# Softmax sums gathered by DMA to 128x64, inverted there and spread back to the denominators' rows, with a new order of the fill

## The chip, the core and the metric

The kernel is one program on one core of a Trainium2 chip. The metric is device time in microseconds, from launch to the end of the last store; less is better. The core has a matrix engine (TensorE, PE in the rows; PEld is its weight loading), three engines for elementwise work (VectorE is DVE, ScalarE is ACT, GpSimd is POOL), a queue engine that issues the transfers (SyncE, SP), and 16 DMA engines that carry them. All engines run at once and wait for each other by semaphores. Each engine takes its own instructions strictly in the order in which they are written.

## The reference, cut to what matters

One transformer block, post-norm, on x of 32 x 256 x 128 in float32: 16 heads of width 8, a causal mask with a linear decay, and a gated feed-forward part with three more layers of width 512.

```python
Q, K, V = (split_heads(x @ W.T + b) for W, b in ((Wq, bq), (Wk, bk), (Wv, bv)))
scores = einsum('bhid,bhjd->bhij', Q, K) / sqrt(8)
scores = where(causal_mask, -inf, scores) - delta      # delta = i - j
out = einsum('bhij,bhjd->bhid', softmax(scores, axis=-1), V)
x = layernorm(x + out @ Wo.T + bo)
h = silu(tlin(x, w1)) * tlin(x, w2)
h = gelu(tlin(gelu(tlin(h, h1)), h2))                  # exact gelu
x = layernorm(x + tlin(h, w3))
```

## The kernel before, in words

The 32 sequences are taken two at a time: 16 pairs, `q` = 0 to 15, of 512 tokens; `b` is the sequence within the pair. Work on one pair is a chain of steps, and the kernel runs three pairs staggered: in **slot** t (t = 2 to 15) the attention of pair t runs beside the projection and the gate layers of pair t-1 and the wide layers of pair t-2. Before the slots stands a **fill** (pairs 0 and 1 from nothing), after them a **drain**. For every engine there is a hand-written list of steps for the fill (`PE_FILL`, `ACT_FILL`, ...), for a slot (`PE_ORDER`, ...; the last number in an entry is the pair relative to t) and for the drain. The lists are unrolled in that order, so they alone decide what stands behind what on an engine.

The steps that matter here, by their names in the lists:

- `qq`, `qk`, `qv`: projections of x, all in one PSUM bank. `qhi`, `qlo` split q and k into a rounded part and a remainder; `qstack`, `kstack` are the seven transfers that lay these parts into the stacks `qs`, `ks`, 32 rows a head. For pair 0 they go half by half (seven transfers for b = 0, seven for b = 1).
- `s` (b, n), n = 0 to 7: scores of two heads (L622, L625) into two of four score banks. `smax` (L947) on VectorE takes the row maximum of each; that frees the banks. In the fill, b = 1 of pair 0 and all of pair 1 go one head at a time through two other banks: `s1` (L638, L640) and `smax1` (L959). I call these first-maxima.
- `mT`, `mTc`, `mTl`, `mTd`: the maxima are transposed, split into two parts and sent by DMA into rows of `qs`, so that the next product already has them subtracted.
- `st` (b, n): the scores again, transposed, minus the maximum (L663, L665), into the four banks; `exp` (L798) on ScalarE writes `pt` and frees them; `sel` (L1094) on GpSimd zeroes what the mask forbids.
- `pv` (b, u), u = 0 to 3: `pt` times V and a column of ones (L682), so that the bank holds numerators in its even rows and the row sums in its odd rows, eight copies of each sum. `araw` (L806 on ScalarE or L983 on VectorE) copies the bank to `raw`, 128 x 512.
- `repack` (L557): eight transfers for a pair and half a batch each: odd rows of `raw` to `den`, even rows to `num`, so that numerator and denominator of an element lie in one partition. `arec` (L987) inverts `den` for b on VectorE, 128 x 256; `amul` (L1120) on GpSimd multiplies to `attT`; `wo` (L691) on TensorE is the projection. It waits for both halves of `attT`.
- `res1`, `lnstat`, `rstd`, `lnnorm`, `x1t`, `x1hi`, `x1lo`, `x1c`: residual, layer norm, transpose and splitting.
- `g`, `u` (m = 0 to 3): the two gate layers (L577, L583; in the fill also L579 with the weights' remainder), `tanh`, `gate`, `gmul`, `ghi`, `glo` make the gated product's two parts. `h` (layer, m): the wide layers, four matmuls with the rounded part and four with the remainder; `gelu`, `hhi`, `hlo` (L1140) follow each. `w3h`, `w3l`, `zt`, `res2`, `lnstat 2`, `store` end a pair.

Between fill and slots TensorE reads a flag that says whether the weights have a remainder at all (L761, `lo_flag`); here they have none, and the slots run without these matmuls. The flag needs `w_hi`, `w_lo` and `w_mx`, which split the weights on ScalarE, split on GpSimd and take the largest remainder on VectorE.

`x_tok` and `xT` are the pair's input in its two layouts (`tload`, `xload`).

## Time and profile before

| what | us |
|---|---|
| median of 3 runs (lowest to highest) | 791.47 (790.95 to 791.99) |
| the profiled execution's own time | 791.65 |
| its span, first to last instruction | 789.8 |
| TensorE busy | 730.5 (92%) |
| VectorE busy | 632.0 (80%) |
| ScalarE busy | 553.2 (70%) |
| GpSimd busy | 510.6 (65%) |
| mean granted clock of TensorE | 0.95 of full |

The profiled execution lies within the runs. Busy times are sums over the whole span; they don't say which engine ends a stage. That is read from stretches of the trace and from what ended an engine's idle time. The end of a matmul is modelled: a gap of a few tenths of a microsecond behind one can be covered by it, and then shows only as a late start of the next.

### The profile page before, as it was taken

How to read it: one execution, taken by the hardware profiler on the slowest of the kernel's cores; microseconds unless marked ns; L12 is line 12 of the kernel's file. 1: busy time of each engine (PE TensorE's matmuls, PEld its weight loads, DVE VectorE, ACT ScalarE, POOL GpSimd, SP SyncE). 2: the span in 40 equal slices, each digit the busy share in tenths (PEclk: the TensorE clock that was granted, in tenths of full speed). 3: DMA queues.
4: the chain of work that ended last, by engine and by line, in shares of the span. 5: the costliest groups of instructions: out<-in, count | busy, mean ns of one | idle time of the engine just before them, and what ended most of it. 6: DMA issues, size and time to landing. Idle time of an engine off the chain costs nothing. (4 is left out here: it accounts for less than half of the span.)

```text
span 789.8 us, 18746 instructions
## 1 busy us (share of the span) xinstructions
PE 730.5 (92%) x6026; PEld 500.7 (63%) x6026; DVE 632.0 (80%) x2759; ACT 553.2 (70%) x874; POOL 510.6 (65%) x616
## 2 busy tenths in 40 slices
PE   3587789999999999999999999999999999999995
PEld 1365457676766667676766667676766667676663
DVE  3796679798988979798988979798988979798232
ACT  3154456959687685959687685959687785959684
POOL 2084356766758586766758586766758586767864
PEclk8557699999999999999999999999999999999998
DMA  7311030402112030302112130402112130300100
GB/s 208 138 58 44 0 133 10 140 15 101 55 57 99 34 116 10 139 16 100 55 62 94 39 112 8 139 16 100 55 61 94 41 112 7 127 15 18 40 1 28
DMA packets 36778, 53.28 MB, mean 67 GB/s; under 512 B 5288, under 2 KB 16872, under 8 KB 36680
## 3 DMA queue, kind: packets, MB, share of 16 engines
q1 hardware_dynamic: 36680, 52.07, 19.3%
q8 instruction: 50, 0.82, 0.4%
q14 instruction: 48, 0.39, 0.2%
HBM read 12.20 MB, written 4.19 MB: 21 GB/s over the span
## 5 line engine op out<-in xcount | busy, mean ns | idle before, releaser
L947 DVE CUSTOM_DVE_ANT_0 ps<-ps,causal 128x256 f32<-128x256 f32 (+1 forms) x928 | 297.3, 389 | 22.2 <-PE ps L625 20.4
L798 ACT ACTIVATE pt<-ps 128x768 f32<-128x768 f32 x256 | 195.7, 812 | 37.2 <-PE ps L665 33.6
L1094 POOL TENSOR_SCALAR_AFFINE_SELECT pt<-pt 128x512 f32<-128x512 f32 x256 | 160.3, 637 | 93.5 <-ACT pt L798 89.5
L1140 POOL TENSOR_TENSOR hlo<-hf,hhi 128x512 fp32r<-128x512 f32 x128 | 164.7, 1288 | 85.7 <-ACT hhi L881 85.7
L871 ACT ACTIVATE hf<-ps,vec_sb 128x512 f32<-128x512 f32 x128 | 86.2, 684 | 101.5 <-PE ps L583 100.9
L577 PE MATMUL ps<-hhi,h_hi 128*128 128x512 f32 x496 | 145.8, 415 | 0.3 <-ACT hhi L881 0.3
L583 PE MATMUL ps<-hlo,h_hi 128*128 128x512 f32 x496 | 136.4, 396 | 0.2 <-POOL hlo L1140 0.2
L947 DVE DVE_READ_ACCUMULATOR2_ANT m<- 128x1 f32 x928 | 127.6, 138 | 0.0
L583 PEld LDWEIGHTS ps<-hlo,h_hi 128*128 128x128 f32 x496 | 93.4, 188 | 22.9 <-POOL hlo L1140 0.6
L682 PE MATMUL ps<-pt,vst 128*32 128x256 f32 (+1 forms) x2048 | 106.2, 337 | 1.1 <-POOL pt L1094 1.1
L577 PEld LDWEIGHTS ps<-hhi,h_hi 128*128 128x128 f32 x496 | 85.3, 188 | 22.1 <-issue 3.0
L881 ACT CAST hhi<-hf 128x512 fp32r<-128x512 f32 x128 | 79.3, 620 | 3.9
L622 PE MATMUL ps<-ks,qs 32*128 32x256 f32 x464 | 72.4, 386 | 9.7 <-DVE m L947 8.4
L682 PEld LDWEIGHTS ps<-pt,vst 128*32 128x32 f32 x2048 | 56.1, 111 | 37.7 <-issue 5.3
L1146 POOL TENSOR_TENSOR hlo<-hf,hhi 128x512 fp32r<-128x512 f32 x60 | 76.9, 1282 | 3.3 <-ACT hhi L820 2.5
L622 PEld LDWEIGHTS ps<-ks,qs 32*128 32x128 f32 x464 | 37.9, 185 | 50.6 <-issue 24.5
L663 PE MATMUL ps<-qs,ks 32*128 32x128 f32 x512 | 65.1, 331 | 2.7 <-DMA qs<-mT_lo 1.6
L665 PE MATMUL ps<-qs,ks 32*128 32x256 f32 x512 | 66.5, 340 | 0.0
L663 PEld LDWEIGHTS ps<-qs,ks 32*128 32x128 f32 x512 | 39.7, 189 | 42.2 <-ACT pt L798 22.8
L577 PE MATMUL ps<-x1hi,w_hi 128*128 128x512 f32 x128 | 63.7, 497 | 1.3 <-DVE sg L1024 1.1
L1037 DVE SCALAR_TENSOR_TENSOR hf<-ps,half_s,sg 128x512 f32<-128x512 f32 x60 | 44.9, 748 | 23.4 <-PE ps L583 21.8
L987 DVE RECIPROCAL den<-den 128x256 f32<-128x256 f32 x32 | 55.8, 1745 | 8.2 <-DMA num<-raw 8.2
(116 smaller groups left out, 1154.4 us busy)
## 6 DMA issues: line engine op xcount, KB each, us to landing
qs<-q_hi SPq DMA_DIRECT2D x30, 256.0 KB
ks<-k_hi SPq DMA_DIRECT2D x30, 256.0 KB
xT<-in_x SPq DMA_DIRECT2D x16, 256.0 KB, 2.8
x_tok<-in_xtok SPq DMA_DIRECT2D x16, 256.0 KB, 3.2
den<-raw SPq DMA_DIRECT2D x64, 64.0 KB, 2.0
num<-raw SPq DMA_DIRECT2D x64, 64.0 KB, 2.0
out<-o_tok SPq DMA_DIRECT2D x16, 256.0 KB, 2.0
qs<-q_lo SPq DMA_DIRECT2D x15, 256.0 KB
```

The costliest lines, as they stand in the source:

```text
L577: pe.matmul(acc, w_hi[name][:, col[k]:col[k] + P], hi(k), start=(k == 0), stop=False)
L583: last = pe.matmul(acc, w_hi[name][:, col[k]:col[k] + P], lo(k), start=False, stop=(k == n - 1))
L622: pe.matmul(ps[:, bank, 0:T], qr[:, P:T], kr, start=True, stop=False, skip_group_check=True)
L663: pe.matmul(ps[:, bank, 0:P], kr[:, P:T], qr[:, P:T], start=True, stop=False, skip_group_check=True)
L682: last = pe.matmul(acc, vst[p][:, 2 * b + kb, u, c, :], pr, start=(kb == 0 and not odd), stop=(kb == 1 and odd == 1), skip_group_check=True)
L798: nc.scalar.activation(pt[u][:, c:c + 2, :], ps[:, first:last + 1, 0:3 * P], ACT.Exp).then_inc(t_free.sem, 1)
L871: nc.scalar.activation(hf[:, n % 4, :], ps[:, FB[m % 2], :], ACT.Gelu, scale=vec_sb[:, col:col + 1]).then_inc(f_gelu.sem, 1)
L881: nc.scalar.copy(h_hi[layer % 2][:, m, :], hf[:, n % 4, :]).then_inc(hhi_ready.sem, 1)
L947: part = nc.vector.tensor_tensor_reduce(ps[:, bank, cols], ps[:, bank, cols], mask, 1.0, LOWEST, ALU.add, ALU.max, m32[b][:, it, c + e, u: ...
L1094: nc.gpsimd.affine_select(out=diag, in_=diag, compare_op=ALU.is_ge, fill=0.0, base=0, pattern=[[0, 2], [0, 2], [1, P]], channel_multiplier ...
L1140: nc.gpsimd.tensor_tensor(h_lo[layer % 2][:, m, :], hf[:, n % 4, :], h_hi[layer % 2][:, m, :].bitcast(F32), ALU.subtract).then_inc(hlo_rea ...
L1146: nc.gpsimd.tensor_tensor(lo[:, m, :], gated(q, m), hi[:, m, :].bitcast(F32), ALU.subtract).then_inc(h0lo_ready.sem, 1)
```

## The change

`raw` holds eight copies of each row sum. Before, all eight are moved and all are inverted: a reciprocal over 128 x 256 for each b. Now a `gather` takes every eighth row from row 1 of `raw` for each half, 16 rows of 256 elements, and lays them as 64 x 64 into a new tile `sums` (one for each b, 128 x 64 with two copies of each sum). `arec` inverts `sums`. Four `spread` transfers copy all of `sums` into every fourth row of `den`, once for each residue of the row number. `repack` moves the numerators alone. `araw` waits for repack and gather of the half before it, `arec` for the gather, `spread` for the reciprocal, and `amul` for repack and spread.

The core of the diff (an order table's line or two stand for the tables):

```diff
 SP_ORDER = [
-    ("repack", 0, 1, 0, -1), ("tload", -1), ("repack", 0, 1, 1, -1), ("repack", 0, 0, 0, -1),
+    ("gather", 0, 0, -1), ("gather", 0, 1, -1), ("repack", 0, 0, -1), ("repack", 0, 1, -1),
+    ("spread", 0, 0, -1), ("spread", 0, 1, -1), ("spread", 0, 2, -1), ("spread", 0, 3, -1),
...
+        sums = [sb(f"sums{b}", [P, T // 4]) for b in range(2)]
...
-        repacked = Signal("repacked", 8, 16)
+        gathered = [Signal(f"gathered{b}", 2, 16) for b in range(2)]
+        repacked = [Signal(f"repacked{b}", 2, 16) for b in range(2)]
+        spread = [Signal(f"spread{b}", 4, 16) for b in range(2)]
...
+                    elif kind == "gather":
+                        _, b, half = s
+                        raw_ready.wait(sp, q, b + 1)
+                        spread[b].wait(sp, q - 1)
+                        carry(sp, "sp")
+                        sp.dma_start(sums[b][64 * half:64 * half + 64, :],
+                                     raw[1::8, half * T:(half + 1) * T]).then_inc(gathered[b].sem, 16)
                     elif kind == "repack":
-                        _, b, odd, half = s
+                        _, b, half = s
                         raw_ready.wait(sp, q, b + 1)
                         attT_ready.wait(sp, q - 1, b + 1)
                         carry(sp, "sp")
-                        sp.dma_start((num, den)[odd][64 * half:64 * half + 64, b * T:(b + 1) * T],
-                                     raw[odd::2, half * T:(half + 1) * T]).then_inc(repacked.sem, 16)
+                        sp.dma_start(num[64 * half:64 * half + 64, b * T:(b + 1) * T],
+                                     raw[0::2, half * T:(half + 1) * T]).then_inc(repacked[b].sem, 16)
+                    elif kind == "spread":
+                        _, b, row = s
+                        rec_ready.wait(sp, q, b + 1)
+                        attT_ready.wait(sp, q - 1, b + 1)
+                        carry(sp, "sp")
+                        sp.dma_start(den[row::4, b * T:(b + 1) * T], sums[b][:]).then_inc(spread[b].sem, 16)
...
-                        repacked.wait(dve, q - 1 + b, 8 - 4 * b)
+                        repacked[1 - b].wait(dve, q - 1 + b)
+                        gathered[1 - b].wait(dve, q - 1 + b)
...
-                        repacked.wait(dve, q, 4 * b + 4)
-                        nc.vector.reciprocal(den[:, b * T:(b + 1) * T], den[:, b * T:(b + 1) * T]
-                                             ).then_inc(rec_ready.sem, 1)
+                        gathered[b].wait(dve, q)
+                        nc.vector.reciprocal(sums[b][:], sums[b][:]).then_inc(rec_ready.sem, 1)
...
-                        rec_ready.wait(pool, q, b + 1)
+                        repacked[b].wait(pool, q)
+                        spread[b].wait(pool, q)
```

All order tables are new. The slot's boundary is turned by about one gate block: `u 3`, `gate 3` and `gmul 3` of pair t-1 now stand at the start of slot t+1, while `ghi 1` to `ghi 3`, `araw 1` and the first three `gelu`/`hhi` on ScalarE stand at the end of slot t. On ScalarE, `("table", "exp")` now stands ahead of the first k copy of the fill, and `w_hi 1` behind `qhi 1, 1`; on GpSimd, `w_lo 1` stands behind `sel 0, 4` of pair 1.

TensorE at the start of the fill. L638 and L640 are first-maxima of b = 1, L622 and L625 two-head steps of b = 0 (L643, L646 in the changed file, whose lines lie about 21 further down). Before:

```order
L596 MATMUL ps<-xT,wq_sb 128x512
L638 MATMUL ps<-ks,qs 128x256
L640 MATMUL ps<-ks,qs 128x128
L638 MATMUL ps<-ks,qs 128x256
L640 MATMUL ps<-ks,qs 128x128
L622 MATMUL ps<-ks,qs 128x256 x2
```

After:

```order
L617 MATMUL ps<-xT,wq_sb 128x512
L643 MATMUL ps<-ks,qs 128x256 x2
L646 MATMUL ps<-ks,qs 128x128 x2
L643 MATMUL ps<-ks,qs 128x256 x2
L646 MATMUL ps<-ks,qs 128x128 x2
L643 MATMUL ps<-ks,qs 128x256 x2
```

Three two-head steps of the first half now stand ahead of the first step of the second half.

TensorE at the start of the first slot (every later slot is alike). L577 and L583 with `hhi` and `hlo` are `h 1, 0`; L682 is `pv`. Before, behind the flag:

```order
L622 MATMUL ps<-ks,qs 128x256 x2
L625 MATMUL ps<-ks,qs 128x128 x2
L682 MATMUL ps<-pt,vst 32x256 x4
L682 MATMUL ps<-pt,vst 32x128 x4
L622 MATMUL ps<-ks,qs 128x256 x2
L625 MATMUL ps<-ks,qs 128x128 x2
L622 MATMUL ps<-ks,qs 128x256 x2
L625 MATMUL ps<-ks,qs 128x128 x2
L682 MATMUL ps<-pt,vst 32x256 x4
L682 MATMUL ps<-pt,vst 32x128 x4
L577 MATMUL ps<-hhi,h_hi 128x512 x4
```

After:

```order
L598 MATMUL ps<-x1hi,w_hi 128x512
L604 MATMUL ps<-x1lo,w_hi 128x512
L643 MATMUL ps<-ks,qs 128x256 x2
L646 MATMUL ps<-ks,qs 128x128 x2
L643 MATMUL ps<-ks,qs 128x256 x2
L646 MATMUL ps<-ks,qs 128x128 x2
L703 MATMUL ps<-pt,vst 32x256 x4
L703 MATMUL ps<-pt,vst 32x128 x4
L703 MATMUL ps<-pt,vst 32x256 x4
L703 MATMUL ps<-pt,vst 32x128 x4
L643 MATMUL ps<-ks,qs 128x256 x2
L646 MATMUL ps<-ks,qs 128x128 x2
```

`u 3` has come in front, the first two score steps stand together, and so do the two `pv` steps.

SyncE in a slot, from the first transfer out of `raw`. Before:

```order
L557 DMA den<-raw 64x256
L519 DMA x_tok<-in_xtok 128x512
L557 DMA den<-raw 64x256
L557 DMA num<-raw 64x256 x2
L557 DMA den<-raw 64x256 x2
L557 DMA num<-raw 64x256 x2
L550 DMA qs<-mT_hi 4x4x256
```

After:

```order
L565 DMA sums<-raw 64x1x64 x2
L572 DMA num<-raw 64x256 x2
L579 DMA den<-sums 32x4x64 x4
L565 DMA sums<-raw 64x1x64 x2
L572 DMA num<-raw 64x256 x2
L579 DMA den<-sums 32x4x64 x4
L500 DMA xT<-in_x 128x512
L527 DMA x_tok<-in_xtok 128x512
L558 DMA qs<-mT_hi 4x4x256
```

The four spreads of b = 0 stand ahead of the gathers of b = 1, and the loads of x behind all of them.

## Rows read from the trace of the kernel before

**Rows 1.** The page: TensorE and exp; 40 equal slices, busy and granted clock in tenths.

```profile
PE 730.5 (92%) x6026; PEld 500.7 (63%) x6026; DVE 632.0 (80%) x2759; ACT 553.2 (70%) x874; POOL 510.6 (65%) x616
...
PE   3587789999999999999999999999999999999995
...
PEclk8557699999999999999999999999999999999998
...
L798 ACT ACTIVATE pt<-ps 128x768 f32<-128x768 f32 x256 | 195.7, 812 | 37.2 <-PE ps L665 33.6
```

**Rows 2.** Busy time by stage: stretch, length, engines (instructions), granted clock, DMA share, GB/s.

```profile
0.00:22.80 22.80, 7.71 (x21) 4.09 (x22) 6.47 (x30) 7.99 (x15) 4.90 (x13) 0.83 0.69 206
22.80:80.50 57.70, 42.71 (x345) 30.17 (x344) 47.92 (x253) 23.25 (x35) 27.31 (x32) 0.59 0.21 72
80.50:112.30 31.80, 25.95 (x201) 15.93 (x200) 20.73 (x54) 16.27 (x26) 12.47 (x21) 0.74 0.22 78
112.30:733.90 621.60, 610.51 (x5268) 418.87 (x5268) 538.54 (x2376) 470.48 (x742) 430.94 (x519) 1.00 0.19 66
733.90:789.80 55.90, 43.66 (x196) 31.66 (x196) 18.29 (x46) 35.23 (x58) 34.99 (x34) 0.94 0.04 15
```

**Rows 3.** Timeline of the fifth slot's start: start, length, engine, line, operation [idle before].

```profile
289.82 0.38 PE L622 MATMUL ps<-ks,qs 32*128 32x256 f32 x2
...
291.62 2.62 POOL L1146 TENSOR_TENSOR hlo<-hf,hhi 128x512 fp32r<-128x512 f32 x2
...
291.90 0.38 PE L622 MATMUL ps<-ks,qs 32*128 32x256 f32 x2 [0.48 <-DVE m L947]
...
293.88 1.10 SPq L557 DMA_DIRECT2D den<-raw  x2
294.09 1.10 PE L583 MATMUL ps<-hlo,h_hi 128*128 128x512 f32 x4
...
295.12 0.39 PE L622 MATMUL ps<-ks,qs 32*128 32x256 f32 x4
...
298.36 1.75 DVE L987 RECIPROCAL den<-den 128x256 f32<-128x256 f32 x1
...
300.32 0.75 POOL L1120 TENSOR_TENSOR attT<-num,den 128x256 f32<-128x256 f32 x1
...
302.23 1.16 PE L691 MATMUL ps<-wo_sb,attT 128*128 128x128 f32 x8
```

**Rows 4.** Timeline of the same slot's middle: gate block, transpose, two transposed score steps.

```profile
320.49 0.50 PE L577 MATMUL ps<-x1hi,w_hi 128*128 128x512 f32 x1
...
320.83 0.39 PE L583 MATMUL ps<-x1lo,w_hi 128*128 128x512 f32 x1
...
321.37 0.39 PE L649 MATMUL ps<-ident,m 128*16 128x128 f32 x2 [0.16 <-DVE k_lo L919]
...
321.69 0.33 PE L663 MATMUL ps<-qs,ks 32*128 32x128 f32 x2
...
322.16 0.33 PE L663 MATMUL ps<-qs,ks 32*128 32x128 f32 x2
```

**Rows 5.** The reciprocals' line, and the landing of the transfers of L557.

```profile
L987 DVE RECIPROCAL den<-den x32: 1740/1744/1755, 75.2 to 740.6; 128x256 f32<-128x256 f32 x32
...
DMA to landing us min/median/max: 1.9/2.0/4.2
```

**Rows 6.** Timeline of the fill: half 0's last stack transfer, first scores, last first-maximum, first slot.

```profile
15.17 0.61 SPq L540 DMA_DIRECT2D ks<-k_lo  x1
...
21.96 0.65 PE L638 MATMUL ps<-ks,qs 32*128 32x256 f32 x2 [8.24 <-DMA qs<-no_max]
...
85.68 0.58 PE L638 MATMUL ps<-ks,qs 32*128 32x256 f32 x1
...
112.30 0.38 PE L622 MATMUL ps<-ks,qs 32*128 32x256 f32 x2 [1.09 <-DVE lo_flag L1066]
```

**Rows 7.** The transfers' table: target, source, count, KB, issue to landing in us.

```profile
x<-in_h SPq DMA_DIRECT2D x1, 256.0 KB, 6.7
```

More of the change, by code:

```diff
@@ L91 @@
-    ("exp", 0, 5, 1), ("exp", 0, 6, 1), ("lnnorm", 1, 0), ("x1hi", 0), ("x1c", 0), ("tanh", 0, 0),
-    ("qhi", 0, 2), ("exp", 0, 7, 1), ("tanh", 1, 0), ("qhi", 1, 2), ("ghi", 0, 0), ("tanh", 2, 0),
-    ("ghi", 1, 0), ("exp", 1, 0, 1), ("exp", 1, 1, 1), ("exp", 1, 2, 1), ("tanh", 3, 0), ("exp", 1, 3, 1),
-    ("exp", 1, 4, 1), ("exp", 1, 5, 1), ("exp", 1, 6, 1), ("ghi", 2, 0), ("exp", 1, 7, 1), ("table", "gelu", 1),
+    ("qhi", 0, 0), ("table", "exp", -1), ("qhi", 1, 0), ("rows", 0), ("w_hi", 0), ("qhi", 0, 1), ("qhi", 1, 1),
@@ L95 @@
+    ("lnnorm", 1, 0), ("exp", 1, 0, 1), ("exp", 1, 1, 1), ("x1hi", 0), ("x1c", 0), ("exp", 1, 2, 1),
+    ("exp", 1, 3, 1), ("tanh", 0, 0), ("tanh", 1, 0), ("exp", 1, 4, 1), ("ghi", 0, 0), ("exp", 1, 5, 1),
+    ("tanh", 2, 0), ("exp", 1, 6, 1), ("exp", 1, 7, 1), ("ghi", 1, 0), ("tanh", 3, 0), ("ghi", 2, 0),
+    ("ghi", 3, 0), ("araw", 1, 1), ("gelu", 1, 0, 0), ("hhi", 1, 0, 0), ("gelu", 1, 1, 0), ("hhi", 1, 1, 0),
+    ("gelu", 1, 2, 0), ("hhi", 1, 2, 0),
 ]
 DVE_FILL = [
-    ("rows", 0), ("qlo", 0, 0), ("qlo", 1, 0), ("vadd", 0), ("smax1", 1, 0, 0, 0), ("smax", 0, 0, 0),
@@ L157 @@
+    ("ghi", 0, -1), ("exp", 0, 6, 0), ("exp", 0, 7, 0), ("tanh", 2, -1), ("exp", 1, 0, 0), ("table", "exp", 0),
+    ("exp", 1, 1, 0), ("exp", 1, 2, 0), ("tanh", 3, -1), ("exp", 1, 3, 0), ("exp", 1, 4, 0), ("exp", 1, 5, 0),
+    ("exp", 1, 6, 0), ("exp", 1, 7, 0), ("ghi", 1, -1), ("ghi", 2, -1), ("ghi", 3, -1), ("araw", 1, 0),
+    ("gelu", 1, 0, -1), ("hhi", 1, 0, -1), ("gelu", 1, 1, -1), ("hhi", 1, 1, -1), ("gelu", 1, 2, -1),
+    ("hhi", 1, 2, -1), ("table", "gelu", 0),
 ]
 DVE_ORDER = [
-    ("smax", 0, 0, 0), ("smax", 0, 1, 0), ("smax", 0, 2, 0), ("arec", 0, -1), ("smax", 0, 3, 0),
@@ L201 @@
+    ("ghi", 1, -1), ("tanh", 3, -1), ("ghi", 2, -1), ("ghi", 3, -1), ("table", "exp", 0), ("gelu", 1, 0, -1),
+    ("hhi", 1, 0, -1), ("gelu", 1, 1, -1), ("hhi", 1, 1, -1), ("gelu", 1, 2, -1), ("hhi", 1, 2, -1),
+    ("gelu", 1, 3, -1), ("hhi", 1, 3, -1), ("table", "gelu", 0), ("table", "exp", 1), ("gelu", 2, 0, -1),
+    ("hhi", 2, 0, -1), ("gelu", 2, 1, -1), ("hhi", 2, 1, -1), ("table", "gelu", 1), ("gelu", 2, 2, -1),
+    ("hhi", 2, 2, -1), ("gelu", 2, 3, -1), ("hhi", 2, 3, -1),
 ]
 DVE_DRAIN = [
-    ("arec", 0, -1), ("arec", 1, -1), ("res1", -1), ("lnstat", 1, -1), ("x1lo", -1), ("gate", 0, -1),
```

135 lines of the change are left out of this document (65 added, 70 removed), and 99 rows, old and new, of tables (DVE_FILL, PE_DRAIN, PE_FILL, PE_ORDER).

## The prediction

> **What bounds the kernel now.** I read the head of the page first. TensorE is busy 92% of the span, and the slices show where it is not: the first seven and the last one. The granted clock is at its lower level (1.2 GHz, half) through slices 2 to 4 and full (2.4 GHz) afterwards [rows 1]. The table by stages turns this into three parts [rows 2]: a fill of 112.3 us with 76.4 us of TensorE work, fourteen slots of 44.4 us (621.6 us, 11.1 us idle in all, 0.8 us a slot), and a drain of 55.9 us. VectorE is busy 538.5 of the 621.6 us of the slots, 87%. So the slots are TensorE's. A VectorE instruction that gets cheaper there pays only where TensorE waits for it. The fill is another matter: 36 of its 112 us are idle TensorE and much of the rest ran at half clock.
>
> Some waiting in the slots is hidden, because a matmul's modelled end covers the gap behind it. Two adjacent score steps run side by side in 0.4 us (the row at 295.12, four heads). At a slot's start the step at 291.90 waits 0.48 us for VectorE. In the middle, the step at 321.69 and its partner at 322.16 start 0.47 us apart instead of together, because ScalarE's exp holds the bank, and the transpose at 321.37 comes 0.3 us later than the pace of the two matmuls before it (320.49 and 320.83) allows [rows 3, 4]. I count about 2.5 us a slot of such gaps. That is the most that the slots can give: 35 us.
>
> **The change, part by part.**
>
> 1. *Reciprocals.* 32 at 1.744 us go [rows 5]. Their form after is 128x64. One of 128x4 elements on the same engine is not a reciprocal, so I bound the new one below by a quarter of the old, 0.44 us, and above by the old 1.74; I take 0.5, since the old one costs 6.8 ns an element in its row, far more than any start-up. VectorE sheds 32 x 1.25 = 40 us. In a slot both reciprocals stand behind a score step that VectorE finished and before one that TensorE has not yet delivered: the second ran 298.36 to 300.1, and the next scores came with the pair at 299.42. Nothing in the slots waited for it, so this alone is worth 0 to 0.5 us a slot.
>
> 2. *Eight transfers for b become four plus four, with a reciprocal between.* SyncE issues at 0.55 us each (293.88, two in 1.10) and a transfer lands 2.0 us after its issue, 1.9 at best and 4.2 at worst [rows 3, 5]. Before, raw to attention for the second half took: issue at 293.88, product at 300.32 to 301.1, projection at 302.23 [rows 3]. After, counted from the end of the last score-transposed step of the slot before (st, n=7; 289.82 in these rows): the four pv steps and the moved u(3) put raw at 3.6 to 4.2; the gathers are issued to 5.5 and land at 6.9; the reciprocal ends at 7.4; four spreads are issued by 9.9, the last lands at 11.3; the product follows on GpSimd behind hlo(1,1), 11.55 to 12.3. The projection is due on TensorE at 13.5. The relay is longer by about one landing and eight issues in all, and it is **hidden with 1.4 us to spare**. SyncE issues 30 transfers a slot instead of 22, 17 us of 44; the loads that now stand behind the spreads (x for the next pairs, the maxima, the stacks) are due 5 us or more later. The other half is gathered before the slot turns and its spread lands at 4.6; GpSimd takes it at 7.4. Cost: 0.
>
> 3. *The slot is turned.* u(3), gate, product and hi copy of the fourth gate block cross the slot's boundary. Start of the slot, time 0 as above: pv 0 to 0.79, u(3) to 1.36, s(0),s(1) to 2.0 (the exp of the last bank ends at 1.6), two pv to 3.5, s(2) at 3.65 when VectorE has done s(0) behind the moved product, h(1,0) from 4.0. GpSimd now has three lo parts behind its last masking instead of two: sel to 2.35, then three at 1.23 us to 6.06. In the trace the pair (291.62, 2.62 us) ended at 294.24, just after the matmuls that need it had begun at 294.09 [rows 3]. h(1,0) therefore waits 0.35 us for the third and ends at 6.4. Before, the same work took 5.30 (289.82 to 295.12) plus 1.22 for the pv and u that came ahead: 6.5. Gain 0.1 us. In the middle u(1) moves ahead of g(1), so a block of two matmuls, 0.34 us from 320.49 to 320.83 and some 0.23 for the second, fills the gap before the transpose and the exp wait between 320.83 and 322.16; later two steps wait 0.06 and 0.2 us for exp that did not. Gain 0.3 us. **Slots: 0.4 us x 14 = 5.6 us.** The bounds are -0.8 us a slot (both new waits of 0.35 us, plus one like that at 291.90) and +1.2 (0.1 and 0.3, and the 0.8 us idle of today gone).
>
> 4. *The fill, start.* TensorE's first score step now belongs to half 0, not half 1. Today it waits 8.24 us, to 21.96, for the last of fourteen stack transfers. The seventh, the last of half 0, is issued at 15.17 and finished at 15.78 [rows 6], so it lands at about 17.5. The load of xT for pair 1 is now issued after the five weight loads; the last weight load took 6.7 us to land after an issue at 9.19 (its row gives 6.7) [rows 7], so xT comes near 16.5 and its projection ends at 17.6 to 18.7. I take 18.0 for the first scores: 4.0 us early.
>
> 5. *The fill, until the last first-maximum.* VectorE has 47.9 us of work in the 57.7 us behind 22.8 [rows 2] and is the pacemaker. Doing pair 0's eight two-head steps first, TensorE keeps it fed; of its 9.8 idle us there I give back a quarter, 2.5. The exps of pair 0 begin 6.6 us earlier, the last one 7.5 us earlier. Then some is given back: the second reciprocal waits for pv, raw, the gathers (2.6 us), and its four spreads and product take 4.9 us more before the projection of pair 0. The last first-maximum, at 85.68 today [rows 6], comes at about 81.5: **4.2 us early**.
>
> 6. *The fill, tail.* From that step to the first score step of the slots at 112.30 it takes 26.6 us today [rows 6]. After, VectorE does LN statistics, q_lo, and the maxima's two copies, the transfer lands, and the exps of pair 1's second half start at +7. ScalarE then holds eight exps (0.81 in their row, 0.75 back to back) [rows 1], two copies (1.1), three tanh and a hi copy (2.5), with one 2 us wait for the second gate block, to +19.7; the last g ends at +19.6, the weight flag costs 1.4 (1.09 of it is the wait in the row at 112.30), and u(3) is already in: the slot's s(0) is at +22. Gain 4.6 us. **Fill: 4.2 + 4.6 = about 9 us.** Bounds 3 (the tail gains nothing and one us is lost in 5) and 14 (the 7.5 us are kept). Two extra table loads, 1.28 us each, stand behind raw in the fill and before an exp that is due 2.8 us later: nothing.
>
> 7. *The drain.* Of its 55.9 us TensorE works 43.7 [rows 2]. The third lo part costs h(1,0) 1.2 us where no scores hide it; the projection, which waited 0.44 us for attention, then does not. Together 0 to +1; I take 0.
>
> **Sum** on the profiled execution: 791.65 (span 789.8 and 1.85 around it) - 9 - 5.6 = **777.0 us**. The median of the runs, 791.47, is 0.2 lower, which changes nothing.
>
> **A rule and a row.** The rows have only transfers of 1 KB pieces between on-chip tiles, landing at 2.0 us [rows 5]; gather and spread move pieces of 256 bytes. The Trainium skill, "DMA: Bandwidth & Descriptors", Specifications, says that below 512 B a DMA engine does read-modify-write. The same page, "Why small descriptors are slow (HBM only)", says that copies inside SBUF don't suffer from small descriptors. By the second the sum stands as it is; by the first it is rival B. No row of before tells them apart.
>
> **Rivals.**
> - *A. The slots give nothing.* TensorE is busy 98% of them already, and my 0.4 us is a difference of hidden gaps. 791.65 - 9 = **782.6**.
> - *B. The relay is late, slower than before.* Gather and spread both land x later than 2.0; the projection then waits 2x - 1.4 a slot. It decides from x = 1.25 (landing 3.25 us): 14 x (2.5 - 1.4 - 0.4) = 9.8, about the fill's gain. At 3.6 us it is 14 x 1.4 = 19.6 more, less the fill's 9: **802**. At the row's worst, 4.2, 14 x 2.6 - 9 = +27: 819. For it: the pieces are of a size that no row shows, and 4.2 exists. Against it: 1.9 to 2.0 is the rule for 128 transfers.
> - *C. VectorE's relief pays.* With 2.5 us less work a slot it is always ahead and the gaps of [rows 3, 4] close by half: 1.3 us a slot, 18 us, with the fill's 9: **764.5**.
> - *D. The fill gives nothing and neither do the slots.* TensorE at half clock is busy 42.7 of 57.7 us [rows 2]; if it stays low for longer in the new tail, the same columns take twice the time and the 9 us are gone: **790 to 792**.
>
> **Numbers.** Forecast 0.55, A 0.17, C 0.08, B 0.13 (a third of it between 783 and 792), D 0.07. The range that leaves out C's far end and the heavy part of B is 764 to 788. A measurement of this kernel tells about 0.2% from no change: faster 0.84, same 0.05, slower 0.11.
>
> **What would show it.** Right: reciprocals near 0.5 us; TensorE's first score step at 17.5 to 18.7 instead of 21.96; s(0) of the first slot near 103.5; a slot of 44.0; no wait of the projection (L691 before) for attention in the slots; h(1,0)'s lo matmuls a little late for GpSimd. Wrong: landings over 2.7 us; projections that wait for attT in every slot; VectorE idle before the reciprocals and score steps behind it late; a slot of 44.4 or more; the first slot later than 109.

## The result, and the profile after

| | before | after |
|---|---|---|
| median (lowest to highest), us | 791.46 (790.95 to 791.99) | 779.3 (778.17 to 780.15) |
| ratio, 95% interval | | 0.9845 [0.9828, 0.9863] |
| profiled execution, span | 791.65, 789.8 | 778.17, 776.4 |

The change takes 12.2 us off by the medians, 13.5 us by the profiled executions. The forecast was 777.0 and its range 764 to 788. In what follows *relay* is the chain from `raw` to attention (gather, reciprocal, spread, product), and *the orders* are the new order tables.

The page of the changed kernel, the rows that answer to [rows 1]:

```profile
PE 729.4 (94%) x6025; PEld 497.7 (64%) x6025; DVE 598.0 (77%) x2759; ACT 554.2 (71%) x876; POOL 509.5 (66%) x616
...
PE   3798999999999999999999999999999999999895
...
PEclk8567899999999999999999999999999999999998
```

VectorE has shed 34 us (the 32 reciprocals at 0.55 instead of 1.74 us are 38 us less, other instructions 4 us more), TensorE 1 us. The span has shrunk in the fill: of slices 2 to 6, TensorE is below nine tenths in two instead of five.

Busy time by stage, against [rows 2] (stretch, length, busy time and instructions of PE, PEld, DVE, ACT and POOL, granted clock, DMA share, GB/s). The first two stretches run to the last first-maximum and to the first slot's first scores; the last two are slots and drain:

```profile
22.80:76.10 53.30, 46.46 (x356) 33.68 (x356) 46.15 (x244) 25.59 (x35) 17.63 (x26) 0.63 0.27 84
76.10:101.44 25.34, 22.30 (x176) 11.53 (x176) 16.68 (x41) 13.66 (x23) 16.39 (x22) 0.83 0.24 83
101.44:725.90 624.46, 613.11 (x5304) 420.41 (x5304) 510.07 (x2379) 472.20 (x745) 434.18 (x523) 1.00 0.21 68
725.90:776.40 50.50, 38.40 (x163) 27.68 (x161) 14.89 (x44) 31.85 (x53) 30.25 (x30) 0.95 0.04 14
```

The fill's timeline, against [rows 6] (L617 is a projection, L643 a two-head step, L659 a first-maximum of one head):

```profile
16.10 2.04 PE L617 MATMUL ps<-xT,wq_sb 128*128 128x512 f32 x2 [5.49 <-DMA xT<-in_x]
18.08 0.59 PE L643 MATMUL ps<-ks,qs 32*128 32x256 f32 x4
...
75.94 0.59 PE L659 MATMUL ps<-ks,qs 32*128 32x256 f32 x2
...
80.43 0.60 PE L670 MATMUL ps<-ident,m 128*16 128x128 f32 x2 [1.56 <-DVE q_lo L941]
...
101.44 0.40 PE L643 MATMUL ps<-ks,qs 32*128 32x256 f32 x4
```

First scores 21.96 to 18.08; the last first-maximum 85.68 to 75.94; the first slot 112.30 to 101.44. The fill gives **10.9 us**. Measured from one projection of the attention to the next, a slot was 44.38 us. It is 44.10 now, nine times; the last four are 44.54, 44.66, 44.23 and 44.13. From the first slot's first scores to the last projection inside the slots: 589.4 before, 586.3 now, **3.1 us**. The rest costs **0.6 us** more (88.1, now 88.7). 10.9 + 3.1 - 0.6 = 13.4, the difference of the spans. Of the 3.1 us, 0.6 lie in the first slot up to its projection and 2.5 in the nine even slots; the last four give nothing. The 10.9 us are those of this profiled execution, one of the shorter ones. With the same fill, or nearly the same, the first slot's scores start at 101.3 and 101.8 in two other profiled executions and at 102.4 to 103.0 in four (last section), so the fill's gain lies between 9.3 and 11 us.

The turn of one of the nine slots (start, length, engine, operation, idle before), against [rows 3]:

```profile
496.80 0.55 DVE L1010 RECIPROCAL sums<-sums 128x64 f32<-128x64 f32 x1 [0.57 <-DMA sums<-raw]
498.18 0.75 DVE L1059 SCALAR_TENSOR_TENSOR hf<-ps,half_s,sg 128x512 f32<-128x512 f32 x1 [0.83 <-PE ps L604]
498.48 1.51 PE L703 MATMUL ps<-pt,vst 128*32 128x256 f32 x32
498.82 3.77 POOL L1169 TENSOR_TENSOR hlo<-hf,hhi 128x512 fp32r<-128x512 f32 x3
500.51 0.39 PE L643 MATMUL ps<-ks,qs 32*128 32x256 f32 x2 [0.53 <-DVE m L969]
501.93 1.21 PE L604 MATMUL ps<-hlo,h_hi 128*128 128x512 f32 x4
...
504.21 2.55 SPq L579 DMA_DIRECT2D den<-sums  x4
508.28 0.75 POOL L1143 TENSOR_TENSOR attT<-num,den 128x256 f32<-128x256 f32 x1
510.18 1.16 PE L712 MATMUL ps<-wo_sb,attT 128*128 128x128 f32 x8
```

VectorE waits twice, for the gather and for u(3), then does product and first maximum; s(2) at 500.51 waits 0.53 us for that (0.27 to 0.28 us in the eight even slots before this one). GpSimd's three remainders end at 502.59, which stretches h(1,0)'s remainder matmuls from 1.10 to 1.21 us. The second half's product ends at 509.03, 1.15 us before the projection.

Reciprocals, and the landing of the spreads, against [rows 5]:

```profile
L1010 DVE RECIPROCAL sums<-sums x32: 544/553/554, 60.6 to 724.3; 128x64 f32<-128x64 f32 x32
...
DMA to landing us min/median/max: 1.8/1.8/3.1
```

### The profile page after: what moved, and what is told of

Read it like the earlier page. It is cut to its first block and busy times, and to the rows that moved or that the text cites. A ratio compares the mean times of both kernels' runs of the same rounds, so it can differ in the third digit from the quotient of the medians.

```text
span 776.4 us, 19033 instructions
## 1 busy us (share of the span) xinstructions
PE 729.4 (94%) x6025; PEld 497.7 (64%) x6025; DVE 598.0 (77%) x2759; ACT 554.2 (71%) x876; POOL 509.5 (66%) x616
## 5 line engine op out<-in xcount | busy, mean ns | idle before, releaser
L604 PE MATMUL ps<-hlo,h_hi 128*128 128x512 f32 x496 | 138.7, 398 | 1.7 <-POOL hlo L1169 0.7
L969 DVE DVE_READ_ACCUMULATOR2_ANT m<- 128x1 f32 x928 | 131.0, 141 | 0.0
L643 PE MATMUL ps<-ks,qs 32*128 32x256 f32 x464 | 66.5, 388 | 9.0 <-DVE m L969 9.0
L643 PEld LDWEIGHTS ps<-ks,qs 32*128 32x128 f32 x464 | 34.6, 185 | 54.4 <-DVE m L969 26.6
L1059 DVE SCALAR_TENSOR_TENSOR hf<-ps,half_s,sg 128x512 f32<-128x512 f32 x60 | 44.6, 743 | 10.9 <-PE ps L604 7.6
L604 PE MATMUL ps<-x1lo,w_hi 128*128 128x512 f32 x128 | 50.6, 395 | 0.0
```

The costliest lines, as they stand in the source:

```text
L604: last = pe.matmul(acc, w_hi[name][:, col[k]:col[k] + P], lo(k), start=False, stop=(k == n - 1))
L643: pe.matmul(ps[:, bank, 0:T], qr[:, P:T], kr, start=True, stop=False, skip_group_check=True)
L969: part = nc.vector.tensor_tensor_reduce(ps[:, bank, cols], ps[:, bank, cols], mask, 1.0, LOWEST, ALU.add, ALU.max, m32[b][:, it, c + e, u: ...
```

## The experiments

**Which part of the change pays.** The first run keeps all new orders and puts the old relay back:

```diff
-                        sp.dma_start(sums[b][64 * half:64 * half + 64, :],
-                                     raw[1::8, half * T:(half + 1) * T]).then_inc(gathered[b].sem, 16)
+                        sp.dma_start(den[64 * half:64 * half + 64, b * T:(b + 1) * T],
+                                     raw[1::2, half * T:(half + 1) * T]).then_inc(gathered[b].sem, 16)
...
-                        nc.vector.reciprocal(sums[b][:], sums[b][:]).then_inc(rec_ready.sem, 1)
+                        nc.vector.reciprocal(den[:, b * T:(b + 1) * T], den[:, b * T:(b + 1) * T]
+                                             ).then_inc(rec_ready.sem, 1)
```

> The changed kernel's orders with the relay of before: four transfers of 64x256 for each b (the gathers become transfers of the odd rows into den), reciprocals over 128x256, no spreads. My theory (the new order of the fill makes nearly all of the gain, and in the slots VectorE has room except at the turn of the slot): the fill loses about 2.4 us of VectorE work, and in each slot the first reciprocal, 1.2 us longer, stands ahead of the product and of the first maximum, for which s(2) already waits 0.53 us in the changed kernel's trace; of the 1.2 us some 0.55 are today's wait for the gather. So s(2) comes 0.6 us later a slot: 779.3 + 2 + 14 x 0.6 = about 790. Rival 1 (the relay is a nothing, orders are all): 779 to 781. Rival 2 (the relief of VectorE by 40 us is what pays, orders are nothing): 791 or more, with s(0) of the first slot back near 110; by my theory that s(0) stays below 104.

Measured 791.59 us, ratio 1.0003 [0.9994, 1.0013]: the orders alone give nothing in the end. The trace shows two opposite things. The fill keeps most of its gain: the first slot's scores start at 103.36. The ordinary slots are 44.36 us, as before (two are 44.74 and 45.01). The last three slots are 47.44, 47.06 and 45.48, and there VectorE waits for the first transfers out of `raw` (one row of an ordinary slot, one of a long one):

```profile
547.31 1.75 DVE L997 RECIPROCAL den<-den 128x256 f32<-128x256 f32 x1 [0.78 <-DMA den<-raw]
...
593.48 1.75 DVE L997 RECIPROCAL den<-den 128x256 f32<-128x256 f32 x1 [2.38 <-DMA den<-raw]
```

In the first two of these the granted clock also fell to its lower level, from 598.2 to 601.6 and from 645.9 to 649.4, behind such a wait; where that happens a slot loses about 1.5 us more (the run with four more transfers, below, shows the price). So the turned slot needs the short reciprocal. Of the 0.28 us that an ordinary slot gained, 0.02 come from the order and 0.26 from the relay. My theory had the sum nearly right (790) for partly wrong reasons: the ordinary slots lost 0.26 us instead of 0.6, the last three 7.0 us together, 3 of them by the clock.

The second run is the opposite: the kernel before, with the new relay and the first reciprocal moved to the head of VectorE's slot list (and ahead in its fill). The diff shows the slot list's line only.

```diff
 DVE_ORDER = [
-    ("smax", 0, 0, 0), ("smax", 0, 1, 0), ("smax", 0, 2, 0), ("arec", 0, -1), ("smax", 0, 3, 0),
+    ("arec", 0, -1), ("smax", 0, 0, 0), ("smax", 0, 1, 0), ("smax", 0, 2, 0), ("smax", 0, 3, 0),
```

> The kernel before with the new relay and as little moved as it needs: gather, repack and spread in the places of the old transfers, the reciprocal of b = 0 at the head of VectorE's slot list, and in the fill behind mTl(0,1). My theory (VectorE's relief alone pays little; the second half's product then ends near 302.5 on the old trace's clock, where the projection is due at 302.23): slots within 0.4 us of 44.38, the fill 0 to 2 us shorter, 788 to 795. Rival (VectorE's relief pays): slots of 43.1 to 43.8 us, 772 to 784.

Measured 860.59 us (1.0862 [1.0832, 1.0892]), slots of 46.2 to 51.3 us. Both expectations missed it by far. A typical slot of its trace:

```profile
402.86 0.50 PE L643 MATMUL ps<-ks,qs 32*128 32x256 f32 x2 [1.27 <-DVE m L969]
...
415.29 0.72 POOL L1143 TENSOR_TENSOR attT<-num,den 128x256 f32<-128x256 f32 x1 [2.44 <-DMA den<-sums]
416.17 1.13 PE L712 MATMUL ps<-wo_sb,attT 128*128 128x128 f32 x8 [1.37 <-POOL attT L1143]
```

With the reciprocal at VectorE's head, the first maxima wait for a gather; with its spreads late, product and projection wait. The granted clock is at its lower level in fourteen short stretches of these slots. The three slots without one are 46.2 to 46.4 us long, those with one 47.7 and more, so some 22 of the 70 us are the clock's (an estimate, 1.5 us for each stretch and 3 for one of double length). How much of the rest belongs to my placing of the reciprocal and how much to any relay in the old order isn't separated by this run. VectorE is busy 33 us less in it (599.2 against 632.0), and in this order that is worth nothing.

**Is it VectorE's time or the 64 KB transfers?** The changed kernel, with another reciprocal behind each gather:

```diff
+                        attT_ready.wait(dve, q - 1, b + 1)
+                        nc.vector.reciprocal(den[:, b * T:b * T + D], wv_sb[:])
                         nc.vector.reciprocal(sums[b][:], sums[b][:]).then_inc(rec_ready.sem, 1)
```

> The changed kernel with one more reciprocal (128x128, of the projection's weights, into a part of den that the spreads overwrite) between the gather's landing and each reciprocal, so that VectorE spends about 1.55 us on each b, near the 1.74 of before, with the new transfers unchanged. It tells whether the difference between 791.6 (old relay, new orders) and 779.3 is VectorE's time or the 64 KB transfers of the old relay. Theory V (VectorE's time at the head of the slot): ordinary slots 44.3 to 44.4, the late slots 46 to 47, the fill 1.5 to 2 us longer: 788 to 791. Theory T (the transfers): slots 44.1 to 44.2, 779 to 782. Here the second half's attention is also 1 us later, which the 1.15 us of slack should cover.

Measured 793.88 us (790.69 to 796.22), 3 us above theory V's range and 12 above theory T's. The last four slots are 46.52, 45.32, 45.62 and 45.76; the others 44.1 to 44.9. From the first projection of the slots to the drain's this run takes 627.2 us, the run with the old relay 627.2 and the changed kernel 616.6. No projection of the slots waits for attention. So it is VectorE's time at the reciprocals (theory V) and not the transfers, and it costs most where the gather is late (in the slot of 46.52 the granted clock also fell, from 552.2). The run lengthens both reciprocals of a slot; which of the two costs how much isn't separated.

**The start of the fill.** The changed kernel with the old first part of the fill, and then the kernel before with the new first part (the tables up to the first transpose of the maxima are exchanged):

```diff
 PE_FILL = [
-    ("qq", 0), ("qk", 0), ("qv", 0), ("qq", 1), ("s", 0, 0, 0), ("s", 0, 1, 0), ("s", 0, 2, 0),
+    ("qq", 0), ("qk", 0), ("qv", 0), ("qq", 1), ("s1", 1, 0, 0, 0), ("s1", 1, 0, 1, 0), ("s", 0, 0, 0),
...
 SP_FILL = [
-    ("wload", 0), ("xload", 1), ("qstack", 0, 0), ("kstack", 0, 0), ("kstack", 1, 0), ("qstack", 1, 0),
+    ("xload", 1), ("wload", 0), ("qstack", 0, 0), ("kstack", 0, 0), ("kstack", 1, 0), ("qstack", 1, 0),
```

> The changed kernel with the start of the fill as before: x for pair 1 loaded first, first-maxima of b = 1 ahead of the two-head steps of b = 0, up to the first transpose of the maxima; everything behind it unchanged. First scores should come at 22 us again, instead of 18.08. My theory (VectorE paces the fill up to the last first-maximum, so what the start loses is lost): +4 us, 783. If the exps begin 6.6 us later as I predicted for the change, +6.6: 786. Rival (later waits swallow it, the gain of the fill comes from behind 40 us): 779 to 780.

> The kernel before, old relay and old slots, with only the start of the fill of the changed kernel: weights' first loads before x of pair 1, two-head steps of b = 0 first, up to the first transpose of the maxima, and ScalarE's list up to the second weight split. The converse run (the changed kernel with the old start) lost 5.5 us and began its exps 6.05 us later. Theory S (the start's gain is kept whole through the fill, whatever follows): exps at 42 instead of 48.2, slots begin 5 to 6 us earlier, 785 to 786. Rival (the rest of the old fill's order can't use it, VectorE or ScalarE take it back): 788 to 791.

With the old start 784.82 us (5.5 us lost): first scores at 21.97, first exp at 47.94 instead of 41.89, last first-maximum at 81.93 instead of 75.94, first slot at 107.43 instead of 101.44. The 3.9 us at the first score grow to 6 us at the first exp, and nothing is given back behind it. The new start alone, on the kernel before:

```profile
17.47 0.59 PE L622 MATMUL ps<-ks,qs 32*128 32x256 f32 x4
...
43.26 1.57 ACT L798 ACTIVATE pt<-ps 128x768 f32<-128x768 f32 x2 [10.85 <-PE ps L665]
...
107.76 0.38 PE L622 MATMUL ps<-ks,qs 32*128 32x256 f32 x2 [1.09 <-DVE lo_flag L1066]
```

786.01 us, 5.0 us faster than before (0.9934 [0.9919, 0.9949]), and the first slot 4.5 us earlier. About half of the fill's gain comes from the order of its start, and that half needs no relay.

**How much does the relay have to spare?** Four small transfers ahead of the second half's spreads (the tile, its signal and the gather's wait for them are left out here):

```diff
+                        if (b, row) == (1, 0):
+                            extra.wait(sp, q - 1)
+                            for r in range(4):
+                                sp.dma_start(pad_t[32 * r:32 * r + 32, :], sums[b][32 * r:32 * r + 32, 0:32]).then_inc(extra.sem, 16)
```

> The changed kernel with four small transfers (32 x 32 elements each, into a tile that nobody reads) issued ahead of the spreads of b = 1, so these come about 2.2 us later. It measures the relay's slack. In the trace of the changed kernel the second product ends at 509.03 where the projection starts at 510.18: 1.15 us to spare in an ordinary slot. So the projection waits 2.2 - 1.15 = 1.05 us a slot: 779.3 + 14.7 = 794, and the products are named as what the projection waits for. Rival S (there is more slack than the row shows, since GpSimd only took the product late): 779 to 783. Rival B (the relay binds already, each us of it counts): 779.3 + 31 = 810.

Measured 824.97 us (1.0411), slots of 45.4 to 48.2 us; the four issues took 2.49 us. One slot:

```profile
211.39 0.72 POOL L1151 TENSOR_TENSOR attT<-num,den 128x256 f32<-128x256 f32 x1 [2.40 <-DMA den<-sums]
212.08 2.51 POOL L1171 TENSOR_TENSOR hlo<-hf,hhi 128x512 fp32r<-128x512 f32 x2
212.26 1.13 PE L720 MATMUL ps<-wo_sb,attT 128*128 128x128 f32 x8 [1.38 <-POOL attT L1151]
...
213.70 1.20 PE L606 MATMUL ps<-hhi,h_hi 128*128 128x512 f32 x4
```

The wait of 1.38 us is what 1.15 us of slack leaves of 2.5. But most slots are 2.8 us or more longer. It isn't the two remainders that stand behind the product in GpSimd's queue (212.08): h(2,0) starts 1.44 us behind the projection's start, as in the changed kernel (1.46 us, 511.64 behind 510.18). It is TensorE's clock. Here is the slot up to this projection and the one behind it (same columns as in the table by stage):

```profile
165.37:212.26 46.89, 44.89 (x376) 30.63 (x377) 36.47 (x169) 33.62 (x53) 30.65 (x38) 0.96 0.21 67
212.26:258.22 45.96, 43.36 (x376) 29.55 (x377) 36.93 (x173) 33.55 (x53) 30.61 (x38) 1.00 0.22 69
```

TensorE needs 1.5 us more for the same 376 instructions where the granted clock is 0.96: it is at its lower level (1.2 GHz) from 166.7 to 170.1, right behind a projection that had waited 1.72 us. It fell so behind eleven of the fourteen projections of the slots, all of which had waited 1.35 us or more, and in no slot of the changed kernel. Without their projection's wait, the ordinary slots are 44.0 us long where the clock stayed and mostly 45.5 us where it fell. So the relay is hidden by 1.15 us, a microsecond beyond that costs one, and 1.5 us a slot come on top where the wait is followed by a fall of the clock.

**What binds at the turn.** Three runs. First, a shortened third remainder (the rest of it is left out, so this kernel only measures):

```diff
+                            w = 64 if m == 3 and 1 <= q < LAST - 1 else TOK
-                            nc.gpsimd.tensor_tensor(lo[:, m, :], gated(q, m), hi[:, m, :].bitcast(F32),
+                            nc.gpsimd.tensor_tensor(lo[:, m, :w], gated(q, m)[:, :w], hi[:, m, :w].bitcast(F32),
```

> The changed kernel in which GpSimd takes the remainder of the fourth gate block over 64 of its 512 columns only (pairs 1 to 13; the rest of that block's remainder is left out, so about a microsecond of GpSimd goes at each turn of the slot). It prices the third lo part at the slot's start. My prediction's step 3 said that h(1,0) waits 0.35 us a slot for it: then 779.3 - 14 x 0.35 = 774.4. My reading of the changed kernel's trace (h(1,0)'s remainder matmuls last 1.21 us instead of 1.10, so the wait is 0.11; s(2)'s wait of 0.53 us for VectorE stays): 777.8. If VectorE's product and maximum bind alone: 779.3.

775.72 us, slots of 43.80 instead of 44.10: 0.30 us a slot, near the 0.35 of the prediction and not the 0.11 that I had read from a stretched group of matmuls.

Second, VectorE's maximum ahead of the product and, on ScalarE, raw's copy ahead of the hi copy (the same swap in the fill isn't shown):

```diff
-    ("gate", 3, -2), ("arec", 0, -1), ("gmul", 3, -2), ("smax", 0, 0, 0), ("smax", 0, 1, 0), ("smax", 0, 2, 0),
+    ("gate", 3, -2), ("arec", 0, -1), ("smax", 0, 0, 0), ("gmul", 3, -2), ("smax", 0, 1, 0), ("smax", 0, 2, 0),
...
-    ("exp", 1, 6, 0), ("exp", 1, 7, 0), ("ghi", 1, -1), ("ghi", 2, -1), ("ghi", 3, -1), ("araw", 1, 0),
+    ("exp", 1, 6, 0), ("exp", 1, 7, 0), ("ghi", 1, -1), ("ghi", 2, -1), ("araw", 1, 0), ("ghi", 3, -1),
```

> The changed kernel with two swaps at the turn of the slot: on VectorE the first maximum ahead of the product of the fourth gate block, on ScalarE raw's copy ahead of that block's hi copy. In the changed kernel's trace s(2) waits 0.53 us in every slot for the maximum, which stands behind the product. Theory P (the last of GpSimd's three lo parts, done 2.7 us after the turn's first scores end, is the bound just behind, so nearly all of it is lost again on the lo matmuls of h(1,0)): gain 0.15 us a slot, 777. Theory V (only VectorE's order binds): 0.5 us a slot, 772. Rival against both (raw is no earlier and the product late: the second half's attention comes late): 779 or more.

781.94 us, slots of 44.30, slower: s(2) waits 0.18 us in nearly every slot instead of 0.28 (0.53 in the slot shown above, which isn't the usual one), but hi copy and remainder of the product's block come later, and h(1,0) waits for both. The wait of s(2) was not the bound; the chain behind the product was.

Third, the reciprocal moved out of the way, and with it SyncE's second gathers ahead of the first spreads, two moves in one run:

```diff
-    ("gate", 3, -2), ("arec", 0, -1), ("gmul", 3, -2), ("smax", 0, 0, 0), ("smax", 0, 1, 0), ("smax", 0, 2, 0),
+    ("gate", 3, -2), ("gmul", 3, -2), ("smax", 0, 0, 0), ("arec", 0, -1), ("smax", 0, 1, 0), ("smax", 0, 2, 0),
...
-    ("spread", 0, 0, -1), ("spread", 0, 1, -1), ("spread", 0, 2, -1), ("spread", 0, 3, -1),
-    ("gather", 1, 0, -1), ("gather", 1, 1, -1), ("repack", 1, 0, -1), ("repack", 1, 1, -1),
+    ("gather", 1, 0, -1), ("gather", 1, 1, -1), ("spread", 0, 0, -1), ("spread", 0, 1, -1),
+    ("spread", 0, 2, -1), ("spread", 0, 3, -1), ("repack", 1, 0, -1), ("repack", 1, 1, -1),
```

> The changed kernel with the reciprocal of b = 0 behind the first maximum of the slot instead of ahead of the product, and on SyncE the gathers of b = 1 ahead of the spreads of b = 0. In the last five slots the gather of b = 0 lands 3.3 us after its issue instead of 1.8, and VectorE, whose list has the reciprocal ahead of product and maximum, waits 2.1 us; these slots are 1.1 us longer in sum. Theory G (that wait is what they lose): these slots come back to 44.1, and the others stay, 778.2, if the second half's attention, which now has about 0.1 us to spare, is in time. Theory H (it isn't: SyncE's queue is the relay's bound): projections wait 0.3 to 1 us a slot, 783 to 793. No difference: 779.3.

789.7 us, slots of 44.75 and two late ones of 45.9 and 46.5 (in the second of them the granted clock fell, from 564.3, behind a projection that had waited 1.67 us). The time is theory H's: the relay is late here. A product waits 1.6 us on average for its spreads and the projection 0.62 us a slot. That SyncE's queue is the reason, and not the later reciprocal, is argued; the run moved both.

**A version with one remainder moved.** In the changed kernel ScalarE is idle for 0.85 us ahead of its last four exps and GpSimd for 0.5 us ahead of its last two maskings (less than the 1.3 and 2.3 us of my expectation). One of the three remainders goes there:

```diff
-    ("exp", 1, 6, 0), ("exp", 1, 7, 0), ("ghi", 1, -1), ("ghi", 2, -1), ("ghi", 3, -1), ("araw", 1, 0),
+    ("ghi", 1, -1), ("exp", 1, 6, 0), ("exp", 1, 7, 0), ("ghi", 2, -1), ("ghi", 3, -1), ("araw", 1, 0),
...
-    ("sel", 1, 4, 0), ("sel", 1, 5, 0), ("sel", 1, 6, 0), ("sel", 1, 7, 0), ("glo", 1, -1),
+    ("sel", 1, 4, 0), ("sel", 1, 5, 0), ("glo", 1, -1), ("sel", 1, 6, 0), ("sel", 1, 7, 0),
```

> The changed kernel with the hi copy of gate block 1 ahead of the last two exps on ScalarE (idle there for 1.3 us) and its remainder ahead of the last two maskings on GpSimd (idle there for 2.3 us), so that two remainders instead of three stand at the turn of the slot. Shortening one of the three gave 0.30 us a slot. If GpSimd's queue at the turn is what that run measured, this gives the same without leaving anything out: slots 43.8, 775.5. Rival (the copy delays the last exps, pv and raw's second copy, and the relay has 1.15 us at most): 779 to 785.

Measured 777.2 us (775.35 to 777.47), ratio to before 0.9825 [0.9811, 0.9838]. The turn of a slot:

```profile
494.90 1.27 POOL L1169 TENSOR_TENSOR hlo<-hf,hhi 128x512 fp32r<-128x512 f32 x1
496.13 1.22 POOL L1116 TENSOR_SCALAR_AFFINE_SELECT pt<-pt 128x512 f32<-128x512 f32 x2
497.33 2.51 POOL L1169 TENSOR_TENSOR hlo<-hf,hhi 128x512 fp32r<-128x512 f32 x2
...
498.42 0.39 PE L643 MATMUL ps<-ks,qs 32*128 32x256 f32 x2 [0.16 <-DVE m L969]
```

Ordinary slots are 43.80 us as in the shortened run, with nothing left out. The interval overlaps the changed kernel's (0.9828 to 0.9863), so the 2 us by the medians aren't shown by the times alone; the trace's slots, 0.3 us shorter in most of them and 2.6 us in sum, bear them out. The fill's projection moved behind the first two score steps added nothing:

> The same, and in the fill the projection of pair 1 behind TensorE's first two score steps instead of ahead of them. In the changed kernel's trace that projection runs 16.10 to 18.14 after a wait for x, and the first scores follow at 18.08; half 0's last stack transfer is issued at about 15.2 and lands near 17.4. Theory S (the start is kept whole): up to 0.6 us more than the run beside it, 775. Rival (VectorE's q and k remainders of pair 1, which stand among the first maxima, then come late): 0 to 1 us more.

777.1 us; first scores at 17.87 instead of 18.29, first exp at 41.90, which is where it was.

**Why the last slots are longer.** In the changed kernel's trace the second transfer of the first gather lands at 3.1 to 3.4 us in the last four slots, at 1.7 to 1.9 in the others; in the kernel before, where nobody waits for it, the worst landing of that line grows from 2.6 to 4.2 us in the same part of the run. A packet of the instruction queue stands beside it. The transfers' table of the 4 us behind the gather's issue in the first of the late slots has this row (packets, MB, share of the 16 engines), and the reciprocal waits:

```profile
q8 instruction: 1, 0.02, 1.4%
```

```profile
542.41 0.55 DVE L1010 RECIPROCAL sums<-sums 128x64 f32<-128x64 f32 x1 [2.11 <-DMA sums<-raw]
```

The same table of the slot before has no such row in the first 2.7 us, and the reciprocal waited 0.57 us. There are three packets of 16 KB in a slot, so their place drifts slowly against the work. This run, on the version with the early remainder, moves them:

```diff
+            for _ in range(128):
+                pe.sem_inc(shifted, 1)
             pe.wait_ge(pool_const, POOL_CONSTS)
```

> The kernel with the early remainder and, at the very start of TensorE's program, 128 instructions that only add to a counter nobody reads (TensorE is idle there for the first 5 us). In the traces the last five slots' first gather lands at 3.1 to 3.4 us, and in each of them a packet of the instruction queue q8 (16 KB, 0.9 to 1.4 us on its engine) runs 1.5 to 2 us behind the gather's issue; in the earlier slots it runs 4 us or more behind and the gather lands at 1.8 to 2.3. There are three such packets in a slot, so 128 more instructions ahead should move them some 7 us earlier against the slot's work. Theory I (the fetch of code makes the gather late): in the last five slots the gather lands at 1.8 to 2.3 again, VectorE waits 0.6 us instead of 2, the slots are 43.8 throughout, 775.3. Rival (something else comes late there, as the loads or the store): landings and slots as they were, 777.2. A third way: the packets now fall on other slots' gathers or on the fill, and the time is the same or up to 2 us worse with the late landings in other slots.

The third way came out. At the turns of the last four slots VectorE's first wait is 0.54 to 0.58 us; in the same version without the 128 instructions it was 0.55 and then 1.8 to 2.3. The long waits now stand in the second and third slot and at the second gather of the eighth, where a packet starts about 1 us behind the issue of the gather's second transfer (slots of 45.04, 44.52 and 45.27 us):

```profile
159.39 0.55 DVE L1013 RECIPROCAL sums<-sums 128x64 f32<-128x64 f32 x1 [1.78 <-DMA sums<-raw]
...
431.48 0.55 DVE L1013 RECIPROCAL sums<-sums 128x64 f32<-128x64 f32 x1 [2.69 <-DMA sums<-raw]
...
644.38 0.55 DVE L1013 RECIPROCAL sums<-sums 128x64 f32<-128x64 f32 x1 [0.57 <-DMA sums<-raw]
```

The late landings followed the packets. The run's own time, 793.15 us, is mostly the price of the 128 instructions: the first matmul starts at 20.66 instead of 5.62 us, and the first projection of the slots 14.1 us later.

## Why the prediction was right, point by point

The time fell into the range. The relay, the early start and the third remainder were right as mechanisms. That the sum came near the time is partly luck: the slots gave 2.5 us less than forecast, and in the fill two larger errors went in opposite directions (5 and 6).

1. *Reciprocals, 0.5 us.* 0.55 measured. "Alone worth 0 to 0.5 us a slot": beside the new orders, the run with the old relay shows 0.26 in an ordinary slot and 1.3 to 2.8 in each of the last three, in two of them 1.5 of it the clock's. The sum had it at zero, which was wrong.
2. *The relay, hidden with 1.4 us to spare.* Every step stands within 0.25 us of its forecast: time 0 is 496.61 in the turn above, the reciprocal ends at 7.5 (7.4 forecast), the spreads are issued by 10.15 (9.9), the product ends at 12.4 (12.3), the projection starts at 13.6 (13.5). To spare: 1.15. What the step lacked is the price behind the slack: the wait itself, and about 1.5 us a slot where it is followed by a fall of the clock. (Its heading has eight transfers for b before; they were four for each b, eight for a pair. Its count of 22 and 30 is right.)
3. *The slot turned, 0.4 us.* 0.28 in nine slots. At the start s(2) came at 3.9 (3.65 forecast), the scores behind h(1,0) started at 6.45 (6.4), and the third remainder was worth 0.30 (0.35 forecast). What failed is whose gain it is: by the order alone a slot gains 0.02 us. And the step knew nothing of the late landings, which take 1.1 us back in the last four slots. Slots: 3.1 instead of 5.6 us, within the bounds given.
4. *The fill's start, first scores at 18.0.* 18.08. The projection ahead of them ended at 18.14, inside the 17.6 to 18.7 forecast.
5. *Last first-maximum at 81.5, 4.2 us early.* It came at 75.94, **9.7 us early**; this term was mis-sized most. The first exp came 6.3 us early, as forecast (6.6). The mistake was the giving back: I let VectorE wait for the second gather and for the spreads. The second reciprocal runs at 67.35 without any wait, eight single maxima behind the first one, and only the projection waits, 0.62 us. The two runs on the start show that 4.5 to 6 us came from the start alone and stayed. The old relay in the new fill puts the last first-maximum 2.3 us later, so the relay has its share too.
6. *The tail, 22 us.* 25.5 us, **3.5 us longer**. I followed ScalarE's chain, but ScalarE was busy only 13.7 us of it. TensorE was busy 22.3 of the 25.3 us, at half clock for the first part:

```profile
76.10:85.20 9.10, 7.37 (x42) 2.50 (x42) 7.96 (x26) 1.38 (x3) 8.94 (x12) 0.52 0.11 41
85.20:101.44 16.24, 14.93 (x143) 9.03 (x134) 8.72 (x16) 12.29 (x21) 7.45 (x11) 1.00 0.31 107
```

   The transpose at 80.43 also waits 1.56 us for VectorE. My reading of [rows 1] had the lower clock in slices 2 to 4 only; in the kernel before it came back in the tail, as it does here, and the step gave it no term. How much of the 3.5 us is the clock's and how much TensorE's load isn't separated. Steps 5 and 6 missed in opposite directions, 5.5 and 3.5 us, and so the fill's 9 came out as 10.9. That is luck, and so is part of the nearness: the fills of other executions end up to 1.8 us later.
7. *The drain, 0 to +1.* +0.6: h(1,0) waits 0.65 us for the third remainder, and the projection 0.69 us for attention, which I had said it would not.

*Rivals.* A (slots give nothing) is refuted for this kernel, but with the old relay it holds for the ordinary slots (44.36 us), and the late ones lose. B (small pieces land late): gather and spread land at 1.8 us, less than the 2.0 of the 1 KB pieces, though they also carry fewer bytes (16 and 32 KB against 64). The Trainium skill, "DMA: Bandwidth & Descriptors", section "Why small descriptors are slow (HBM only)", says that copies within SBUF don't suffer from small pieces, and the trace agrees; the rule in its Specifications on pieces below 512 B shows no price here. Still B's mechanism was the near miss, for another reason: a gather that lands 1.3 to 1.6 us late beside a packet of the instruction queue took back 1.1 us of the gain. B's prices (802, 819) also leave out the fall of the clock: of the 46 us that the run with four more transfers lost, 24 are waits of the slots' projections and some 16 the clock's (eleven falls of 1.5 us). C (1.3 us a slot from VectorE's relief) and D did not happen.

## What to carry to other kernels

Price a shorter instruction and a new order together: here neither the relay in one placing (860 us) nor the orders (791.6 us) gave anything alone, and both gave 12 us. A gain at the very start of a fill can be kept whole if the engine that sets the pace starts earlier, as it was here, so look there before the steady state. A transfer that an in-order engine waits for needs slack for its worst landing. Missing it costs the wait, and, if TensorE stands still meanwhile, perhaps a stretch at the lower clock behind it: read the granted clock slot by slot before you look for queues.
